# Expert stages of a two-attention, two-expert block: order of the router's last products, and banks of the second down projection

## The reference

```
inh     = sigmoid(y @ Wr / temperature)                       # 8 experts
near    = exp(-|inh - 1/e| / 0.1) where inh is in the zone, else 0
far     = exp(-|inh - 1/e| / 0.3) on the best two experts, normalised
weights = near, or far where near is 0 for all; normalised
out     = sum over e of weights[e] * ((silu(y @ Wg[e]) * (y @ Wu[e])) @ Wd[e])
x       = x + out
```

## Time and profile before

| | us |
|---|---|
| median of the runs | 1679.6 (1679.0 to 1680.09) |
| profiled execution, its own time | 1678.52 |
| its span, first to last instruction | 1676.5 |
| TensorE busy | 1560.3 (93%) |
| VectorE busy | 1134.7 (68%) |
| ScalarE busy | 863.2 (51%) |
| GpSimd busy | 635.3 (38%) |
| first expert stage, start of TensorE's first product | 477.39 |
| second expert stage, the same | 1389.60 |

### The profile page before, as it was taken

The page is one execution under the profiler, slowest core; times in us unless marked ns, Lnnn a source line. Parts: engine busy times, 40 slices in busy tenths (PEclk is TensorE's granted clock), DMA queues, the critical chain, the costliest instruction groups (busy, mean ns, idle before and its releaser), DMA issues. The chain is left out here.

```text
span 1676.5 us, 29418 instructions
## 1 busy us (share of the span) xinstructions
PE 1560.3 (93%) x9784; PEld 1353.0 (81%) x9784; DVE 1134.7 (68%) x2542; ACT 863.2 (51%) x2140; POOL 635.3 (38%) x543
## 2 busy tenths in 40 slices
PE   6698889988979999996999999999999998999998
PEld 4577778777768888885888888888888886888887
DVE  6677777777776555566677677777767788555554
ACT  3365556655643333324677676667767653333332
POOL 2666666666510000004565566556555630000000
PEclk9799999999999999998999999999999999999999
DMA  2100000000011000001000000000000001000001
GB/s 92 45 16 16 15 8 15 7 15 8 1 45 38 20 20 19 1 1 57 7 20 7 19 6 25 19 6 19 6 19 6 1 1 39 19 20 20 19 0 51
DMA packets 11645, 32.24 MB, mean 19 GB/s; under 512 B 1200, under 2 KB 5296, under 8 KB 11568
## 3 DMA queue, kind: packets, MB, share of 16 engines
q1 hardware_dynamic: 11568, 31.28, 5.7%
HBM read 29.18 MB, written 2.10 MB: 19 GB/s over the span
## 5 line engine op out<-in xcount | busy, mean ns | idle before, releaser
L378 POOL TENSOR_TENSOR ab_swapped<-ab_swapped,const 128x512 f32<-128x512 f32 x128 | 169.1, 1321 | 236.3 <-ACT ab_swapped L373 236.0
L1553 DVE TENSOR_TENSOR f_hidden<-ps,f_silu 128x512 f32<-128x512 f32 x128 | 87.6, 689 | 202.0 <-PE ps L116 202.0
L1443 ACT ACTIVATE f_silu<-ps 128x512 f32<-128x512 f32 x128 | 76.3, 598 | 283.0 <-PE ps L116 283.0
L114 PE MATMUL ps<-xh,f_wl 128*128 128x512 f32 x512 | 203.2, 397 | 1.5 <-DVE f_hidden L1553 1.5
L115 PE MATMUL ps<-xl,f_wh 128*128 128x512 f32 x512 | 202.8, 396 | 0.0
L116 PE MATMUL ps<-xh,f_wh 128*128 128x512 f32 x512 | 202.6, 396 | 0.0
L1272 POOL TENSOR_TENSOR ab_qk<-ab_qk,ab_swapped 128x512 f32<-128x512 f32 x128 | 173.7, 1357 | 10.0
L378 DVE TENSOR_TENSOR ab_qk<-ps,const 128x512 f32<-128x512 f32 x128 | 88.0, 688 | 108.8 <-PE ps L116 108.8
L621 ACT ACTIVATE aa_probs<-ps,aa_negmax 128x256 f32<-128x256 f32 x256 | 119.6, 474 | 78.8 <-DVE aa_negmax L701 74.9
L1064 ACT ACTIVATE ab_probs<-ab_probs,ab_negmax 128x128 f32<-128x128 f32 (+1 forms) x256 | 114.5, 449 | 78.5 <-DVE ab_negmax L1162 77.9
L114 PE MATMUL ps<-f_wh,f_hl 128*128 128x256 f32 x512 | 144.4, 282 | 3.3 <-DVE x L1569 3.3
(11 more groups left out here) (188 smaller groups left out, 4640.8 us busy)
## 6 DMA issues: line engine op xcount, KB each, us to landing
f_stage<-wf_in SPq DMA_DIRECT2D x16, 768.0 KB, 4.2
b_stage<-wb_qkv_in SPq DMA_DIRECT2D x8, 768.0 KB, 4.2
a_stage<-wa_in SPq DMA_DIRECT2D x7, 320.0 KB, 2.9
x<-x_in SPq DMA_DIRECT2D x4, 512.0 KB, 7.0
bo_stage<-wb_out_in SPq DMA_DIRECT2D x8, 256.0 KB, 2.6
out<-x SPq DMA_DIRECT2D x4, 512.0 KB, 2.9
a_stage<-wa_in SPq DMA_DIRECT2D x7, 288.0 KB, 2.8
const<-const_in SPq DMA_DIRECT2D x1, 704.0 KB, 5.3
```

The costliest lines, as they stand in the source:

```text
L114: nc.tensor.matmul(out, ll, rh, start=start, stop=False)
L378: return engine.tensor_tensor(by_batch(out), by_batch(src), table(c, rows, col), ALU.mult)
L1443: nc.scalar.activation(silu[:, m, :], GATE(m), ACT.Silu).then_inc(silu_done, 1)
L1553: nc.vector.tensor_tensor(hidden[:, m, :], UP(m), silu[:, m, :], ALU.mult).then_inc(hid_done, 1)
```

## The change

In both expert stages the opening is reordered. TensorE does the router products of groups 0 to 2, the first half (m = 0) of the first gate and up, the transposes of the last group, the second half, and only then the router products of the last group and the transposes of the logits. ScalarE and VectorE take the first group's silu, hidden rows and splits ahead of the router's exponentials and distances; VectorE splits the first weights before it finishes the last group's rows. The last group's transposes go to banks 6 and 7, and the router products alternate between banks 4 and 5, with a wait for the copy. The second down projection (n = 1) goes to banks 6 and 7 and waits for no addition; the third (n = 2) waits for the first and second addition count.

```diff
--- before.py
+++ after.py
@@ -1304,9 +1304,10 @@
         out_ready, out_added, stored = sem("out_ready"), sem("out_added"), sem("stored")
         GATE = lambda m: c.ps[:, 2 * m, :]
         UP = lambda m: c.ps[:, 2 * m + 1, :]
-        OUT = lambda i: c.ps[:, 4 + i, :].rearrange("p (t d) -> p t d", d=D)
-        norm_banks, own_banks = [c.ps[:, 6, :], c.ps[:, 7, :]], [GATE(1), UP(1)]
-        PRODUCTS = lambda s: c.ps[:, 4 + s, :]
+        SECOND = 1
+        OUT = lambda n, i: c.ps[:, (6 if isinstance(n, int) and n == SECOND else 4) + i, :].rearrange("p (t d) -> p t d", d=D)
+        norm_banks = own_banks = [c.ps[:, 6, :], c.ps[:, 7, :]]
+        PRODUCTS = lambda s: c.ps[:, 4 + s % 2, :]
         LOGITS = c.ps[:, 4, 0:NT * 2 * E].rearrange("p (t w) -> p t w", w=2 * E)
         TURNS = E // 2
         block = ctx.enter_context(nc.Block())
@@ -1341,19 +1342,13 @@
 
         @block.tensor
         def _(pe):
-            def router_products():
-
-                for s in range(NG):
-                    if s == 1:
-                        norm_turn(nc, c, own_norm, pe, NG - 1, own_banks)
-                    if s == NG - 1:
-
-                        pe.wait_ge(own_norm.lo_done, KD * NG)
-                    g = slice(s * G, (s + 1) * G)
-                    for k in range(KD):
-                        nc.tensor.matmul(PRODUCTS(s), c.wr[:, k, :], c.xl[:, k, g], start=(k == 0), stop=False)
-                        ins = nc.tensor.matmul(PRODUCTS(s), c.wr[:, k, :], c.xh[:, k, g], start=False, stop=(k == KD - 1))
-                    ins.then_inc(products_ready, 1)
+            def router_products(s):
+                after(pe, flat_done, s - 1)
+                g = slice(s * G, (s + 1) * G)
+                for k in range(KD):
+                    nc.tensor.matmul(PRODUCTS(s), c.wr[:, k, :], c.xl[:, k, g], start=(k == 0), stop=False)
+                    ins = nc.tensor.matmul(PRODUCTS(s), c.wr[:, k, :], c.xh[:, k, g], start=False, stop=(k == KD - 1))
+                ins.then_inc(products_ready, 1)
 
             def router_turn():
 
@@ -1362,12 +1357,12 @@
                     ins = nc.tensor.transpose(LOGITS[:, t, :], flat_logits[:, t * P:(t + 1) * P], c.ident[0:2 * E, 0:2 * E])
                 ins.then_inc(logits_ready, 1)
 
-            def gate_up(it, e, s, first=False):
+            def gate_up(it, e, s, first=False, halves=(0, 1)):
                 n = 8 * it + 4 * e + s
                 if s == 0:
                     pe.wait_ge(w_lo, 2 * it + e + 1)
                 g = slice(s * G, (s + 1) * G)
-                for m in range(2):
+                for m in halves:
                     if not first:
 
                         pe.wait_ge(hid_done, 2 * n + m - 1)
@@ -1385,13 +1380,16 @@
 
                     pe.wait_ge(chained, 2)
                 for i in range(2):
-                    if not first:
+                    if isinstance(n, int) and n == SECOND + 1:
+
+                        pe.wait_ge(out_added, i + 1)
+                    elif not (first or isinstance(n, int) and n == SECOND):
 
                         pe.wait_ge(out_added, 2 * n + i - 1)
                     for t in range(2):
                         tok = slice((2 * i + t) * P, (2 * i + t + 1) * P)
                         for k in range(KD):
-                            ins = matmul3(nc, OUT(i)[:, t, :], (hh[:, s % 2, k, tok], hl[:, s % 2, k, tok]), (wh[:, e, 2, k, :], wl[:, e, 2, k, :]), k == 0, k == KD - 1)
+                            ins = matmul3(nc, OUT(n, i)[:, t, :], (hh[:, s % 2, k, tok], hl[:, s % 2, k, tok]), (wh[:, e, 2, k, :], wl[:, e, 2, k, :]), k == 0, k == KD - 1)
                     ins.then_inc(out_ready, 1)
 
             def turn(it, first, last):
@@ -1404,9 +1402,15 @@
                         if last and e == 1 and s in (1, 3) and norm:
                             norm_turn(nc, c, norm, pe, s // 2, norm_banks)
 
-            router_products()
+            for s in range(NG - 1):
+                router_products(s)
+            gate_up(0, 0, 0, True, (0,))
+            norm_turn(nc, c, own_norm, pe, NG - 1, own_banks)
+            gate_up(0, 0, 0, True, (1,))
+
+            pe.wait_ge(own_norm.lo_done, KD * NG)
+            router_products(NG - 1)
             router_turn()
-            gate_up(0, 0, 0, True)
             turn(0, True, False)
             with pe.Fori(1, TURNS - 1) as it:
                 turn(it, False, False)
@@ -1414,10 +1418,9 @@
 
         @block.scalar
         def _(act):
-            def router_flat():
-                for s in range(NG):
-                    act.wait_ge(products_ready, s + 1)
-                    nc.scalar.copy(flat_logits[:, s * G:(s + 1) * G], PRODUCTS(s)[0:2 * E]).then_inc(flat_done, 1)
+            def router_flat(s):
+                act.wait_ge(products_ready, s + 1)
+                nc.scalar.copy(flat_logits[:, s * G:(s + 1) * G], PRODUCTS(s)[0:2 * E]).then_inc(flat_done, 1)
 
             def router_exps():
 
@@ -1450,26 +1453,33 @@
                     act.wait_ge(out_ready, 2 * (n - 1))
                 nc.scalar.copy(hh[:, s % 2, m, :], hidden[:, m, :]).then_inc(hi_done, 1)
 
-            def turn(it, last):
+            def turn(it, first, last):
                 for e in range(2):
                     for s in range(NG):
-                        activate(it, e, s, 0)
-                        activate(it, e, s, 1)
-                        hidden_hi(it, e, s, 0)
-                        hidden_hi(it, e, s, 1)
+                        if not (first and e == 0 and s == 0):
+                            activate(it, e, s, 0)
+                            activate(it, e, s, 1)
+                            hidden_hi(it, e, s, 0)
+                            hidden_hi(it, e, s, 1)
                         if s == 1 and not (last and e == 1):
                             split_hi(*((it, 1) if e == 0 else (it + 1, 0)))
                         if last and e == 1 and s == 2 and norm:
                             norm_hi(nc, c, norm, act, 0, norm_banks)
 
             split_hi(0, 0)
+            for s in range(NG - 1):
+                router_flat(s)
+            activate(0, 0, 0, 0)
             norm_hi(nc, c, own_norm, act, NG - 1, own_banks)
-            router_flat()
+            activate(0, 0, 0, 1)
+            router_flat(NG - 1)
+            hidden_hi(0, 0, 0, 0)
+            hidden_hi(0, 0, 0, 1)
             router_exps()
-            turn(0, False)
+            turn(0, True, False)
             with act.Fori(1, TURNS - 1) as it:
-                turn(it, False)
-            turn(TURNS - 1, True)
+                turn(it, False, False)
+            turn(TURNS - 1, False, True)
             if norm:
                 norm_hi(nc, c, norm, act, 1, norm_banks)
 
@@ -1566,7 +1576,7 @@
                     dve.wait_ge(out_ready, 2 * n + i + 1)
                     for t in range(2):
                         at = s * TG + 2 * i + t
-                        ins = nc.vector.scalar_tensor_tensor(out=c.x[:, at, :], in0=OUT(i)[:, t, :], scalar=col[:, e, at:at + 1], in1=c.x[:, at, :], op0=ALU.mult, op1=ALU.add)
+                        ins = nc.vector.scalar_tensor_tensor(out=c.x[:, at, :], in0=OUT(n, i)[:, t, :], scalar=col[:, e, at:at + 1], in1=c.x[:, at, :], op0=ALU.mult, op1=ALU.add)
                     ins.then_inc(out_added, 1)
 
             def take_weights(it, e):
@@ -1582,10 +1592,11 @@
             def turn(it, first, last):
                 for e in range(2):
                     for s in range(NG):
-                        hidden_rows(it, e, s, 0)
-                        hidden_rows(it, e, s, 1)
-                        hidden_lo(it, e, s, 0)
-                        hidden_lo(it, e, s, 1)
+                        if not (first and e == 0 and s == 0):
+                            hidden_rows(it, e, s, 0)
+                            hidden_rows(it, e, s, 1)
+                            hidden_lo(it, e, s, 0)
+                            hidden_lo(it, e, s, 1)
                         if s == 1 and not (last and e == 1):
                             split_lo(*((it, 1) if e == 0 else (it + 1, 0)))
                         if last and e == 1 and s == 2 and norm:
@@ -1602,9 +1613,13 @@
                         if last and e == 1 and s in (1, 3) and norm:
                             normalise(s // 2)
 
+            split_lo(0, 0)
             norm_rows(nc, c, own_norm, dve, NG - 1)
-            split_lo(0, 0)
+            hidden_rows(0, 0, 0, 0)
             norm_lo(nc, c, own_norm, dve, NG - 1, own_banks)
+            hidden_rows(0, 0, 0, 1)
+            hidden_lo(0, 0, 0, 0)
+            hidden_lo(0, 0, 0, 1)
             router_distances()
             turn(0, True, False)
             with dve.Fori(1, TURNS - 1) as it:
```

## The result

The changed kernel takes 1684.15 us (median of eight runs, 1682.65 to 1686.62), the kernel before 1679.3 beside it (1677.45 to 1680.43). The ratio is 1.0029, interval 1.0018 to 1.0040: slower, by 4.9 us; the forecast was 4.0 (1683.6 against 1679.6). The profiled execution is 1684.62 us, its span 1682.6, against 1676.5 before.

What follows compares the result with a forecast made beforehand. TensorE, full mid-stage, keeps whatever a stage's opening loses, and VectorE's queue delays it there. 1679.6 + 2.5 for the later fourth gate and up in both stages + 1.5 for one clock fall = 1683.6 us; range 1680 to 1687.

Steps and rivals of the forecast that it cites:

- TensorE to the logits: Stage opening on TensorE up to the second gate and up: starts at 492.08 against 493.00, 0.9 us won.
- The table loads: ScalarE's function tables: three loads per stage instead of one, 1.28 us each, all hidden and costed at nothing.
- VectorE's chain: VectorE from the distances to the third group's hidden rows: 492.82 to 512.24, against 509.34 for those hidden rows before.
- The loss at the fourth gate and up: TensorE in the opening: fourth gate and up starts at 512.99 against 511.72, losing 1.27 and 1.20 us per stage.
- The waits, foretold as 1.9 and 2.1: TensorE waits for hidden rows before the third and fourth gate and up, replacing waits of 0.76 and 1.44 us.
- 35.5 us after the stage's first product: Sign to look for: where the fourth gate and up starts on TensorE; earlier than 34 us would prove the forecast wrong.
- The clock: TensorE behind the second new wait: falls to half about evenly per stage, +1.5 us in all, bounds 0 and 3.1.
- one fall: Clock at half behind the second wait in one of two stages: 1683.6 us; one fall or two, chance 0.38.
- The row behind the even chance: Trace of TensorE idling 2.26 us between dense products, then half clock for 3.4 us, 1.5 us lost.
- The banks: Second down projection in its own two banks no longer waits for an addition: the 1.44 us wait is gone.

Runs made afterwards that it cites:

- VectorE's order: Changed kernel with picks, router weights and additions moved behind later groups' hidden rows on VectorE: 1676.08 us, ratio to before 0.9985.
- the first pick: Changed kernel with VectorE's router work moved behind hidden rows, but one of two picks ahead of the second group's hidden rows: 1674.3 us, ratio to before 0.9971.
- the wait filled: Changed kernel with eight unread 512-column products on TensorE ahead of each stage's fourth gate and up: 1680.84 us, ratio to before 1.0012.
- the second measurement: The changed kernel measured again without a further edit: 1684.19 us.
- the banks alone: Kernel before with only the second down projection moved to banks 6 and 7, without its wait for an addition: 1678.78 us, again 1677.7 us.

## Why the prediction was right

Right in direction and in the mechanism at the openings; near in size, partly by luck.

*TensorE to the logits.* Forecast 492.08 for the second gate and up, with a start at 477.39; measured 492.17 with 477.65. Every wait costed as met was met. From the stage's first product it is 14.52 against 14.69, mostly the transposes of the last group, which took 0.80 and not 0.95; over the six openings it is 13.90 to 14.66, by how long the clock is at half at the start.

*The table loads.* Costed at nothing. In the changed kernel that holds: three loads, the second done 0.4 us before z. The figure of 2.66 us for a switch in the Trainium skill's "ScalarE: Activation LUTs", section "What ACT_TABLE_LOAD costs", would have put the exponential at 494.8, an estimate; it started at 493.76, and load and silu are 1.30 apart (483.62, 484.92), so the trace does not agree. That the third load is free was true only of that order of VectorE: with the picks out of the way it cost 1.32.

*VectorE's chain.* 492.82 to 512.24 in the forecast, 492.80 to 512.23 measured. This is the step that decided the sign, and VectorE's order and the first pick show it from the other side: the same TensorE order is 8 to 10 us faster once hidden rows do not stand behind router work; its two openings together are 6.8 and 10.2 us shorter.

*The loss at the fourth gate and up.* Forecast 1.27 and 1.20 us; measured 1.00, 0.48 and 1.13 in the first stage, 1.11, 0.97 and 0.75 in the second, 0.9 on average. The term was a little large, since how long the clock is at half at the stage's start differs by execution. The waits, foretold as 1.9 and 2.1, read 1.47 and 1.89: I counted from the moment at which a next product could have started, the profile from the modelled end of the last one, and the first stage began 0.26 later than in the profile of before, its VectorE work less so. The starts that end the waits were met (502.4 and 512.99 against 502.37 and 512.97). The sign "35.5 us after the stage's first product" should read 35.6 by the prediction's own sum (512.99 less 477.39).

*The clock.* Forecast: about even in each stage, 1.5 us a fall. Measured: three of six, 10.11 less 8.57 = 1.54 a fall; with the wait filled no fall came in two openings. The case "one fall" was the average, not the rule: none, one and two all occurred. The row behind the even chance was a weaker parallel than the prediction has it. Ahead of that wait of 2.26 us TensorE had idled 5.14, done seven products at half clock and only five at full, not a long dense stretch:

```profile
769.56 0.79 PE L114 MATMUL ps<-xh,ab_wl 128*128 128x512 f32 x1 [5.14 <-DVE ab_wl L1143]
...
772.69 0.39 PE L115 MATMUL ps<-xl,ab_wh 128*128 128x512 f32 x1
```

The price of a fall held; that about half the waits bring one was a guess that came out.

*What was not in the sum.* The part between the openings is 0.5 to 1.8 us longer in the changed kernel's profiles, 1.3 on average, at a lower granted clock in attention b, without an edit there. The first stage also began 1.1 later on average, most of it in one profile. With the openings, 3.6 longer where the forecast had 4.0, this comes to the 5.9 by which the three profiled spans of the two kernels differ. The medians differ by less, 4.9 in the result and 5.5 in the second measurement; the profiled executions of before were shorter than its median. The forecast had one term a little too large and lacked another, and that it lies within a microsecond of the result is partly luck. What causes the missing term is not shown.

*The banks.* Worth in the openings what the earlier trace rows say, where the addition was the last wait: 1.4 to 2.1 us per opening when they are the only edit, though the medians do not show it. In the changed kernel they save what the later additions would cost, and the fourth gate and up waits behind them instead.

## What to carry to other kernels

Work that is moved into one engine's wait has to be followed on the engine that it pushes back. Here 5.6 us of TensorE work ahead of the logits started a 19 us chain of VectorE 6 us later, and TensorE paid for it twice. Separate banks let an addition come late; the gain is only there if the order on the adding engine uses it and puts what TensorE waits for first. A wait of 2 us on TensorE may cost 1.5 more behind it. And at differences of 0.3% a part of the kernel that nobody edited can differ too: read it, with its granted clock, before all of a difference is put down to the edit.

## What the runs showed of the hardware

Equal idle times of TensorE, 3.42 and 3.44 us, left its clock at full once and at half once; of two waits of 1.87 us in one profile of the changed kernel the first was followed by half clock and the second was not. A half clock behind the wait cost 1.5 us each time. The mean granted clock of a whole execution was 0.985 before and 0.982 to 0.983 with the banks alone, and the windows show part of that difference (0.83 against 0.76 and 0.80 of full clock) in a stage whose code is the same. A VectorE operation of 0.29 us with two inputs in SBUF took 3.20 beside one GpSimd operation that has two as well. A function table load took 1.28 us, its function started 0.02 behind it, and it was free where ScalarE would have waited for data.
